# Quantised attention with keys on partitions, its exponentials copied to whole numbers by GpSimd, and fp8 rows normalised on ScalarE

## The reference, cut to what matters

```python
q = _fq_sym(q * scale, axis=-1)      # s = max|q|/127 per query and head; q = round(q/s)*s
k = _fq_sym(k, axis=-1)
v = _fq_sym(v, axis=2)               # per head and channel, over the keys
attn = softmax(einsum('bhqd,bhkd->bhqk', q, k))
attn = _fq_unsigned(attn, axis=-1)   # s = max(attn)/255 per query; round(attn/s)*s
out = einsum('bhqk,bhkd->bhqd', attn, v) ... @ Wp + bp
```

```python
scale_x = max(max|x| over the whole tensor / 448, 1e-6)
x8 = (x / scale_x).astype(float8_e4m3fn)
```

## Time and profile before

| what | value |
|---|---|
| median of 3 runs | 3404.22 us (3401.59 to 3406.93) |
| the profiled execution: time, span | 3412.33 us, 3410.3 us |
| PE busy | 2727.4 us (80%) |
| DVE busy | 2490.0 us (73%) |
| ACT busy | 1909.4 us (56%) |
| POOL busy | 602.4 us (18%) |
| mean granted TensorE clock | 0.901 |

### The profile page before, as it was taken

How to read it: one execution, slowest core, us unless ns; L and a number is a source line. 1 busy time by engine, 2 the same in 40 slices (tenths; PEclk the granted TensorE clock), 3 DMA queues, 4 the chain that set the end, 5 groups by cost and what they waited for, 6 DMA issues and landing times. The chain is left out here.

```text
span 3410.3 us, 63176 instructions
## 1 busy us (share of the span) xinstructions
PE 2727.4 (80%) x21404; PEld 1416.1 (42%) x21404; DVE 2490.0 (73%) x4757; ACT 1909.4 (56%) x2773; POOL 602.4 (18%) x539
## 2 busy tenths in 40 slices
PE   5768999686799999999996677686789628859983
PEld 3344444333465656565663433333211213334542
DVE  5746677656799999999994666624499796676548
ACT  2554433232599999999992533321578332844541
POOL 4341000012110101010104233303021610020013
PEclk8978999897899999999998888887899859978996
DMA  4433420200000000000000200010332010032301
GB/s 149 170 140 115 155 75 37 90 0 16 19 13 7 13 7 13 7 13 7 7 0 16 87 0 0 18 59 13 75 75 50 22 50 0 1 85 50 67 8 53
DMA packets 65341, 152.00 MB, mean 45 GB/s; under 512 B 11841, under 2 KB 20049, under 8 KB 63377
## 3 DMA queue, kind: packets, MB, share of 16 engines
q1 hardware_dynamic: 62368, 140.43, 13.8%
q0 software_dynamic: 2800, 9.18, 0.8%
HBM read 93.61 MB, written 24.38 MB: 35 GB/s over the span
## 5 line engine op out<-in xcount | busy, mean ns | idle before, releaser
L1617 DVE TENSOR_REDUCE s_top<-ps 128x1 f32<-128x512 f32 x1024 | 657.3, 684 | 30.4 <-PE ps L1512 29.9
L1586 ACT ACTIVATE s_prob<-ps,s_shift,m_sq 128x1024 int16<-128x1024 f32 x512 | 615.1, 1202 | 30.6 <-DVE s_shift L1625 30.6
L1512 PE MATMUL ps<-s_ks,s_qs 128*128 128x512 f16 x1024 | 352.5, 386 | 61.0 <-issue 14.8
L1517 PEld LDWEIGHTS ps<-ident,s_prob 128*128 128x128 f16 x4096 | 272.7, 98 | 123.5 <-DVE m_o L1635 51.5
L1517 PE MATMUL ps<-ident,s_prob 128*128 128x128 f16 x4096 | 314.2, 220 | 0.7 <-ACT s_prob L1586 0.5
L1505 PE MATMUL ps<-s_ks,s_qs 128*128 128x512 f16 x1024 | 307.5, 382 | 1.0 <-ACT s_prob L1586 0.5
L1592 ACT ACTIVATE s_probT<-ps 128x1024 f16<-128x1024 int16 x256 | 262.2, 1024 | 7.0 <-PE ps L1517 6.6
L1008 PE MATMUL ps<-m_hT,m_w 128*128 128x512 f16 x1024 | 232.3, 381 | 1.8 <-PEq L105 1.8
L249 PE MATMUL ps<-ident,s_parts 128*128 128x128 f16 x640 | 77.4, 296 | 129.2 <-POOL s_parts L240 127.5
L1630 DVE CAST s_probT<-ps 128x1024 f16<-128x1024 int16 x256 | 174.4, 681 | 4.7 <-PE ps L1517 4.7
L2289 DVE TENSOR_SCALAR s_prob<-ps,s_cap 128x1024 f32<-128x1024 f32 x128 | 158.2, 1270 | 25.8 <-PE ps L2198 25.8
(11 more groups left out here) (403 smaller groups left out, 5708.5 us busy)
## 6 DMA issues: line engine op xcount, KB each, us to landing
s_qs<-m_qT SPq DMA_DIRECT2D x144, 128.0 KB
s_ks<-m_kT SPq DMA_DIRECT2D x96, 128.0 KB
numbers<-s_numbers SPq DMA_DIRECT2D x21, 512.0 KB, 2.7
s_slabs<-numbers SPq DMA_DIRECT2D x21, 512.0 KB, 5.9
m_ks<-context_parts SPq DMA_DIRECT2D x12, 512.0 KB
expert_rows<-s_y SPq DMA_DIRECT2D x19, 256.0 KB, 2.0
s_rows_in<-in_ctx SPq DMA_DIRECT2D x16, 256.0 KB
x_sb<-in_L_ffn_W_up SPq DMA_DIRECT2D x4, 1024.0 KB, 6.0
```

The lines of the kernel that those rows point to most:

```text
L1512: pe.matmul(quarter_at(q), qs[:, hb, bass.ds(t * P, P)], ks[:, hb, cols(q, 512)], start=True, stop=True).then_inc(s.top_scored, 1)
L1517: j = pe.transpose(turned(half, F16)[:, cols(m, P)], prob[:, u, cols(8 * half + m, P)].bitcast(F16), k.ident[:])
L1586: act.activation(prob[:, u, cols(half, HALF)], pair(half).rearrange("p m n -> p (m n)"), ACT.Exp, bias=shift[:, u:u + 1], scale=sq[:, bass ...
L1617: dve.tensor_reduce(top4[:, u, q:q + 1], quarter_at(q), AX.X, ALU.max).then_inc(s.top_read, 1)
```

## The change

Queries and keys change places. The queries are now kept as two f16 parts like the keys (three stacked products, 96 rows), and the scores come out with 128 keys on partitions and 512 queries in the columns. The unit of work is a step: one tile of 128 keys, one group of 512 queries, four heads; 16 steps make a block and 16 blocks the attention. In a step PE makes four scores and four matmuls for the maxima of a later block (19 steps ahead), and mixes a step that lies two back: values as 32-wide f16 weights against the int16 bits read as f16 (whole numbers times 2^-24), ones as 32-wide f32 weights against the unrounded exponentials. The transposes, the copies out of PSUM and the stage that transposes `o` are gone. The shift (negated top plus ln 255) goes into five extra rows of the query operand through five small DVE operations, a PE transpose, a DVE copy and a DMA. ACT writes exponentials in f32, POOL copies them to int16. At the end of a block ACT copies sums and mix out of PSUM, PE picks the sums onto query partitions, DVE inverts them, PE spreads them again, DVE multiplies, ACT and POOL write two f16 parts into `qT` in place. In fp8_rows ACT normalises once into a buffer (bias and scale) and later scales by the inverse; DVE only reduces and rounds, with two row buffers, and the weights are turned in two halves.

```diff
 def quantised_heads(...)
-                    if scale != 1.0:
-                        v.done(dve.tensor_scalar(inv[:], inv[:], scale, None, ALU.mult))
-                    v.done(dve.tensor_tensor(scaled[...], rows[...], inv[...].broadcast_to([P, H, HD]), ALU.mult))
+                    v.done(dve.scalar_tensor_tensor(scaled[...], rows[...], scale,
+                                                    inv[...].broadcast_to([P, H, HD]), ALU.mult, ALU.mult))
...
+    A = H // DC; ROWS = 3 * HD; BLOCKS = DC * G; KT = T; STEPS = BLOCKS * KT; TILES = A * TG
+    AHEAD = KT + 3; LAG = 2; EVACUATE, PICK, WIDE, HIGH, LOW = 1, 5, 8, 9, 9; END = STEPS + WIDE + 1
...
 sync
+            for a in range(A):
+                queries(0, a, first[a])
+                keys(0, a, first[a])
+            for b in (1, 2):
+                for a in range(A):
+                    queries(b, a, q_loaded[b])
+            for a in range(A):
+                keys(1, a, k_loaded[1])
+            for b in range(BLOCKS):
+                sp.wait_ge(s.top_read, number["shift", b] + 1)
+                sp.dma_start(qs[ROWS:ROWS + SHIFTS, b % 3, :, :], shiftT[:, b % 2, :]).then_inc(shifted[b % 3], 16)
+                if b and b + 2 < BLOCKS:
+                    sp.wait_ge(s.scored, A * KT * b)
+                    for a in range(A):
+                        queries(b + 2, a, q_loaded[(b + 2) % 3])
...
 gpsimd
+            pool.memset(ks[ROWS:ROWS + SHIFTS, :, :, :].rearrange("p u a n -> p (u a n)").bitcast(F32), TWO_SIXTEENS
+                        ).then_inc(s.consts_ready, 1)
+            for n in range(STEPS + KT):
+                if n < STEPS:
+                    if n >= 3:
+                        pool.wait_ge(s.mixed, n - 2)
+                    for a in range(A):
+                        pool.wait_ge(s.exp_ready, A * n + a + 1)
+                        pool.tensor_copy(ints[:, n % 3, a, :], prob[:, n % 4, a, :]).then_inc(s.rounded, 1)
...
 tensor
+            def mix_values(n):
+                b, t = n // KT, n % KT
+                if t == 0 and b:
+                    pe.wait_ge(s.evacuated, 2 * b)
+                pe.wait_ge(s.rounded, A * (n + 1))
+                for a in range(A):
+                    pe.matmul(mixed_at[cols(a, HD), :], values[:, t, cols(b // G * A + a, HD)], ints[:, n % 3, a, :].bitcast(F16),
+                              start=(t == 0), stop=(t == KT - 1))
+            def mix_ones(n):
+                t = n % KT
+                for a in range(A):
+                    j = pe.matmul(sums_at[cols(a, HD), :], ones[:], prob[:, n % 4, a, :],
+                                  start=(t == 0), stop=(t == KT - 1))
+                j.then_inc(s.mixed, 1)
...
+            for m in range(-AHEAD, END):
+                i = m + AHEAD
+                if i == 0:
+                    pe.wait_ge(s.consts_ready, 4)
+                for a in range(A):
+                    if 0 <= m + 1 < STEPS:
+                        score(m + 1, a)
+                    if i < STEPS:
+                        top(i, a)
+                    if a == 0 and LAG <= m < STEPS + LAG:
+                        mix_values(m - LAG)
+                    if a == 1 and LAG <= m < STEPS + LAG:
+                        mix_ones(m - LAG)
+                if i % TILES == 0 and 0 < i <= STEPS:
+                    turn_shift(i // TILES - 1)
+                if m >= KT and m % KT == PICK:
+                    pick_sums(m // KT - 1)
+                if m >= KT and m % KT == WIDE:
+                    spread_inverse(m // KT - 1)
...
 scalar
+            def exp(n, a):
+                g = A * n + a
+                if a == 0 and n >= 4:
+                    act.wait_ge(s.mixed, n - 3)
+                act.wait_ge(s.scored, g + 1)
+                act.activation(prob[:, n % 4, a, :], score_at(g), ACT.Exp).then_inc(s.exp_ready, 1)
+            def evacuate(b):
+                if b:
+                    act.wait_ge(s.lo_ready, b)
+                act.wait_ge(s.mixed, KT * (b + 1))
+                act.activation(sums[:], sums_at, ACT.Copy).then_inc(s.evacuated, 1)
+                act.activation(num[:], mixed_at, ACT.Copy).then_inc(s.evacuated, 1)
...
 vector
+            def shifts(b):
+                dve.wait_ge(s.top_read, number["top", TILES * (b + 1) - 1, 3] + 1)
+                hi, mid, lo = (shift[:, b % 2, r, :] for r in range(3))
+                v.done(dve.tensor_reduce(least[:], ntop[:, b % 2, :, :], AX.X, ALU.min))
+                v.done(dve.tensor_scalar(hi, least[:], 1.0 / SIXTEEN, None, ALU.mult))
+                v.done(dve.scalar_tensor_tensor(rest[:], least[:], 1.0 / SIXTEEN, hi, ALU.mult, ALU.subtract))
+                v.done(dve.tensor_scalar(mid, rest[:], 1.0, None, ALU.mult))
+                dve.tensor_tensor(lo, rest[:], mid, ALU.subtract).then_inc(s.shift_ready, 1)
...
 fp8_rows, scalar
+            for t in range(T):
+                act.wait_ge(s.offset_ready, t // R + 1)
+                act.activation(normal[:, t, :], k.x[:, t, :], ACT.Identity, bias=offset[:, t:t + 1],
+                               scale=k.rstd[:, t:t + 1]).then_inc(s.normal_ready, 1)
+            copy_weights(k, s, act, weights, weight_banks(weights, 0, 2))
+            act.wait_ge(s.inv_ready, 1)
+            act.wait_ge(s.normal_ready, T)
+            for t in range(2 * R):
+                scale_rows(t)
+            copy_weights(k, s, act, weights, weight_banks(weights, 1, 2))
...
 layer1_xattn
-            quantised_heads(k, hT, wq, k.i.L1_xattn_bq, scale, sq=..., ints=qT)
-        o = sb("o", [P, H, T, HD], F32)
-        attention_quantised(k, qT, sq, kT, values, o)
+            quantised_heads(k, hT, wq, k.i.L1_xattn_bq, scale, parts=qT)
+        attention_quantised(k, qT, kT, values)
...
-            transposed_parts(k, oT, tiles=o)
-            project_and_add(k, oT, wp, k.i.L1_xattn_bp, 1)
+            project_and_add(k, qT, wp, k.i.L1_xattn_bp, 1)
```

More of the change, by code:

```diff
@@ L1416, in _ @@
                                   ALU.subtract).then_inc(s.numbers_ready, 1)
[L1419 to L1465, removed]
@@ L1467, in _, with queries @@
         @s.block.sync
         def _(sp):
[L1469 to L1475, removed]
+            def queries(b, a, sem):
+                for r, (lq, _) in enumerate(STACK[0:3]):
+                    sp.dma_start(qs[cols(r, HD), b % 3, a, :], qT[cols(a, HD), lq, b // G, cols(b % G, GT)]).then_inc(sem, 16)
@@ L1490, in _ @@
[L1490 to L1493, removed]
[L1494 to L1499 removed]
+            pool.memset(pick[:], 0.0).then_inc(s.consts_step, 1)
@@ L1567, in _, with bank_free @@
[L1567 to L1578 removed]
+            def bank_free(job):
+                if job >= 3:
+                    pe.wait_ge(s.top_read, job - 2)
@@ new lines, in top @@
+            def top(i, q):
+                b, a, tile = i // TILES, i % TILES // TG, i % TG
+                c = b // G
+                if b == 0 and tile == q == 0:
+                    pe.wait_ge(first[a], 96)
+                if b and i % TILES == q == 0:
+                    pe.wait_ge(q_loaded[b % 3], 16 * 3 * A * ((b - 1) // 3 + 1 if b % 3 else b // 3))
+                    if b % G == 0:
+                        pe.wait_ge(k_loaded[c % 2], 16 * 3 * A * ((c + 1) // 2))
+                job = number["top", i, q]
+                bank_free(job)
+                pe.matmul(top_at(job), qs[0:ROWS, b % 3, a, cols(tile, P)], ks[0:ROWS, c % 2, a, cols(q, GT)],
+                          start=True, stop=True).then_inc(s.top_scored, 1)
@@ L1595, in tile @@
-            def tile(n, u, first):
-                act.wait_ge(s.shift_ready, n + 1)
-                exp(n, u, 0)
-                if not first:
-                    copy(n - 1, (u - 1) % R)
-                exp(n, u, 1)
-            tile(0, 0, True)
-            for n in range(1, 1 + R):
-                tile(n, n % R, False)
-            with act.Fori(0, (NT - 1 - R) // (2 * R)) as i:
-                for a in range(2 * R):
-                    tile(2 * R * i + a + 1 + R, (a + 1) % R, False)
@@ new lines, in hi @@
+            def hi(b):
+                act.wait_ge(s.top_read, number["wide", b] + 1)
+                act.activation(qT[:, 0, b // G, cols(b % G, GT)], num[:], ACT.Copy).then_inc(s.hi_ready, 1)
+            act.wait_ge(s.consts_ready, 4)
+            for n in range(STEPS + KT):
+                if n < STEPS:
+                    for a in range(A):
+                        exp(n, a)
+                if n >= KT and n % KT == EVACUATE:
+                    evacuate(n // KT - 1)
+                if n >= KT and n % KT == HIGH:
+                    hi(n // KT - 1)
```

367 lines of the change are left out of this document (183 added, 184 removed).

## The result

The changed kernel takes 3414.18 us (median of 7 runs, 3410.74 to 3420.97) where the kernel before, in the same session, takes 3404.06 (7 runs): a ratio of 1.0032, interval 1.0021 to 1.0042.

The account below looks back on a forecast made before the run. ScalarE bounds the old tile (3.45 us); PE was to bound the new step (3.25). Attention +35.8, queries +13.6, o's transposition -21.2, fp8 rows -5: +23.2 on 3412.3, less 8.1, gives 3427 us, range 3405 to 3450.

Parts of the forecast that it names:

- constants, first 21 steps: Attention start: GpSimd fills constants, 7.7 us; then 21 steps bound by DVE's maxima plus the first shift's trip, 53.8 us.
- 235 full steps: Attention's main loop: PE bounds each step at 3.25 us (1.76 + 1.08 + 0.41), 763.8 us in all.
- blocks' own PE work: Per attention block, PE's shift transpose, picked sums and spread inverse: 2.3 us, 15 times, 34.5 us.
- evacuation stall: Block end: PE waits for a score bank while ScalarE awaits the last mix and copies; 1.6 us, 15 times, 24 us.
- shift-chain stall: Once a block, five small DVE operations slowed by GpSimd's copies take 2.4 us; PE stalls 1.5 (0.3 to 3), 15 times: 22.
- My estimate of near 40 us: Shift chain's total stall, in place of 22 us, if each of four DVE operations waited a full GpSimd copy of 0.62.
- Queries as two parts: Quantisation before the attention: queries written as two f16 parts like the keys, 16 x 0.66 plus a tail of 3: +13.6 us.
- Transposition of o: Between the attention and the first projection: this stage goes, -21.2 us.
- fp8 rows: Normalising moved to ScalarE: four rounding groups lose 1.98 us each, 3 perhaps lost behind weight copies; -5 us (-9 to +4).
- GpSimd's copy: Attention's f32 to int16 copy, 0.62 us; rival, chance 0.15: from 0.81 GpSimd becomes the bound, 3474 us at 0.87, 3747 at 1.16.
- the rival without gaps: Four f16 values matmuls per step enter and leave the array neatly, 0.22 us for 0.41: -48 us, 3379; chance 0.17.
- Stalls absorbed: Rival at block boundaries: PE's run-ahead covers evacuation and shift chain, up to 46 us goes, about 3387; chance 0.12.

## Why the prediction was right in its direction and wrong in its size

The mechanism was right: PE takes ScalarE's place as the bound, each step gains 0.17, and what surrounds the steps costs more. The attention's terms, as the prediction put them:

| term | forecast, us | measured, us |
|---|---|---|
| constants, first 21 steps | 7.7 + 53.8 = 61.5 | 943.5 - 882.6 = 60.9 |
| 235 full steps | 3.25 each | 3.28 each: +7 |
| blocks' own PE work, 15 | 2.3 each | 0.80 + 1.11 + 0.25 = 2.16: -2 |
| evacuation stall, 15 | 1.6 each | 1.44: -2 |
| **shift-chain stall, 15** | **1.5 each** | **0.59 + 0.16 - 0.25 = 0.50: -15** |
| 18 steps without maxima | 2.5 each | 2.40: -2 |
| last three mixing steps, last block's chain | 4.5 + 7 = 11.5 | 1828.8 - 1818.8 = 10.0: -1.5 |

With the first line's -0.6 that makes the 16.1 by which the attention came out shorter than forecast. (1818.8 is the start of the third last values group. The 0.25 in the blocks' own work is the length of the shift's transposition, L1554, so how the chain's two slow steps divide between it and the stall is an estimate; their sum, 0.75 for 1.7, is measured.) The failed term is the **shift chain**: I gave five small operations 2.4 us, from the row in which one of them takes 0.57 beside a GpSimd instruction, on the ground that GpSimd copies for 2.5 of every 3.25 us. The row was true and the share was nearly true (2.29 of 3.28). The step that failed was to take the share for a chance: the steps are periodic. GpSimd starts when PE's mixes free its ring, the chain's minimum starts 1.8 us behind that, and the chain falls each time on the same spot, the 0.99 us in which GpSimd waits. That it fell there was luck; nothing in the forecast placed it. The price itself was about right for a chain that meets the copies: in the kernel with the moved chain it takes 2.15 us and the step 0.89 more, 13 us in 15 blocks. That the hold exists and that its phase decides is shown four times: one operation at 0.586 when an edit of PE's order shifted the phase, one at 0.519 when GpSimd's burst was made longer, three at more than 0.5 when the chain was moved into it, and one at 5.2 us when the burst had no pause of its own.

The Trainium skill (SBUF — State Buffer, Who interferes with whom) has these operations wait for GpSimd and a reduce not; the traces agree (the maxima stay at 683 ns in the changed kernel and in the one with the moved chain, the minimum at 220 and 207). My estimate of near 40 us from it erred as the 22 did.

Point by point. *Queries as two parts:* +14.8 for +13.6. *Transposition of o:* -21.6 for -21.2. *fp8 rows:* -7.9 in the trace, -7.0 alone, for -5, inside the bounds, and by luck: the rounding groups' own lines, before and after, are

```profile
L2423 DVE TENSOR_SCALAR s_bits<-s_rows x4: 1226/1227/1227, 2774.9 to 2804.5; 128x2048 int32<-128x2048 int32 x4
...
L2460 DVE TENSOR_SCALAR s_bits<-s_rows x4: 1226/1226/1226, 2779.1 to 2801.3; 128x2048 int32<-128x2048 int32 x4
```

Counted from the last offset row the first group starts at 38.1 before and 37.7 after, as forecast; then three intervals, and not four, shrink from 9.87 to 7.4 us, 2.5 each and not 1.98 (the four normalisations, and 0.6 us that DVE waited ahead of them). The 3 us that I had taken off for ScalarE's second eight weight copies are not seen. *GpSimd's copy:* 0.613 for 0.62, so that rival never came near. *Values matmuls:* 0.42 with gaps for 0.41; the rival without gaps falls, and the kernel with the mixes adjacent shows what it would have been worth. The 0.28 that I had estimated from the Trainium skill (TensorE: Matmul & The Clock Gate, Part 3, Measured speedup vs the span model) is not reached between full-width matmuls either (0.42); between the two narrow groups it is 0.23. *Stalls absorbed:* not so. The evacuation's is not absorbed (taking it away gave 21 us), and the chain's is small because the chain is short, not because PE ran ahead of it.

## What to carry to other kernels

When two engines share something and the loop is periodic, don't multiply a price by a busy share: draw one period from the timeline and see where the short operation falls, and expect that a later edit which shifts a phase can bring the hold back. When a bound engine mixes narrow and full-width matmuls, put the narrow ones together. A wait at the head of an in-order queue (here ScalarE's evacuation) belongs where the engine would have been idle anyway and what it waits for is nearly done (0.65 us of waiting in place of 1.90).

## What the hardware showed that I had not expected

- GpSimd's copy from f32 to 16-bit whole numbers, 128x512, takes 0.613 us, as long as the f16 copy of that size (0.611), and follows the one before at 0.56.
- A VectorE operation of 16 columns was held 5.2 us by GpSimd copies in an unbroken run, and 0.55 once the run had gaps. Elsewhere such operations were let in at the end of one copy in the middle of a run: in the kernel with the moved chain three times a block (0.52 to 0.58 us each), with five copies once (0.26), the next one then being held to the run's last copy (0.52). What tells such a boundary from the nine that did not let it in was not tried and stays open; in the long run GpSimd was behind.
- A hold of a small VectorE operation can cost TensorE its clock: after 4.54 us without a matmul in the kernel with two spare copies, the granted clock was 0.50 and matmuls of 512 columns took 0.61 us for 0.38.
- Between full-width and 32-wide matmuls PE loses 0.09 us going in and 0.11 coming out, with f16 weights as with f32.
